# A graph layer on one core: ScalarE's bank clear and VectorE's x sum change places in the step

## The reference

```python
edge_index = jnp.stack([src, dst])
h = jnp.maximum(_layernorm(x, axis=-1), 0.0)          # x: 12500 x 128
# inside the layer, with h in the place of x:
agg_edge = segment_sum(edge_attr, dst, 12500)         # 200000 x 48, dst sorted
collected = concatenate([h, agg_edge], axis=1)        # 176 wide
h1 = silu(collected @ W1 + b1)                        # 256 wide
h2 = silu(h1 @ W2 + b2)
new = h + (h2 @ W3 + b3)
return x + new
```

## Time and profile before

| | |
|---|---|
| Time, median of 3 runs | 332.24 us (332.16 to 332.84) |
| The profiled execution's own time | 331.64 us |
| Its span, first to last instruction | 329.7 us |
| TensorE busy | 311.4 us (94%) |
| VectorE busy | 248.7 us (75%) |
| ScalarE busy | 225.5 us (68%) |
| GpSimd busy | 42.7 us (13%) |
| Mean DMA rate | 161 GB/s |
| Mean granted TensorE clock | 0.990 |

### The profile page before, as it was taken

The page is one execution under the profiler, slowest core; times in us unless marked ns, Lnnn a source line. Parts: engine busy times, 40 slices in busy tenths (PEclk is TensorE's granted clock), DMA queues, the critical chain, the costliest instruction groups (busy, mean ns, idle before and its releaser), DMA issues.

```text
span 329.7 us, 12673 instructions
## 1 busy us (share of the span) xinstructions
PE 311.4 (94%) x4760; PEld 275.2 (83%) x4761; DVE 248.7 (75%) x611; ACT 225.5 (68%) x435; POOL 42.7 (13%) x45
## 2 busy tenths in 40 slices
PE   5767999999999999999999999999999999999994
PEld 5755898889888898889888988898888888898884
DVE  7887877878787878787787778777878686975551
ACT  8864567756776668665875678667856686669752
POOL 4031311001110111011101111011101110111000
PEclk9995999999999999999999999999999999999999
DMA  6993654575447744675367534763467437711112
GB/s 175 305 299 112 195 165 112 179 225 187 114 148 222 218 112 126 213 222 148 101 197 223 176 109 160 223 207 103 141 216 223 134 104 215 221 47 46 32 28 53
DMA packets 79209, 53.04 MB, mean 161 GB/s; under 512 B 2928, under 2 KB 78794, under 8 KB 79184
## 3 DMA queue, kind: packets, MB, share of 16 engines
q1 hardware_dynamic: 79184, 52.70, 53.6%
HBM read 46.29 MB, written 6.40 MB: 160 GB/s over the span
## 4 chain that ended last, share of the span: by engine, by line
PE 79%; DVE 9%; ACT 4%; issue 4%; DVEq 1%; DMA 1%; POOL 1%; SPq 0%; ACTq 0%; POOLq 0%
PE agg_ps L948 18%; PE z L1030 16%; PE z L1014 6%; PE z L994 6%; PE z L1015 5%; PE z L1018 4%; PE agg_ps L965 4%; PE z L999 4%; PE z L1000 4%; PE z L995 4%; PE z L996 4%; PE stage L952 3%; PE tp L978 2%; DVE out_t L829 2%; DVE agg L788 2%
## 5 line engine op out<-in xcount | busy, mean ns | idle before, releaser
L948 PEld LDWEIGHTS agg_ps<-onehot,raw 128*48 128x48 f32 x1568 | 73.1, 125 | 11.7 <-issue 11.7
L650 DVE TENSOR_TENSOR onehot<-window,rel 128x1176 f32<-128x1176 f32 (+1 forms) x57 | 77.2, 1355 | 2.0 <-ACT rel L441 1.2
L948 PE MATMUL agg_ps<-onehot,raw 128*48 128x42 f32 x1568 | 76.8, 214 | 1.7 <-DVE onehot L650 1.7
L952 PE MATMUL stage<-onehot,raw 128*48 128x42 f32 x1560 | 76.5, 214 | 0.0
L952 PEld LDWEIGHTS stage<-onehot,raw 128*48 128x48 f32 x1560 | 72.7, 125 | 0.0
L410 POOL TENSOR_TENSOR rstd<-vareps,minus_half 112x4 f32<-112x4 f32 (+1 forms) x28 | 38.9, 1389 | 260.3 <-DVE vareps L635 260.3
L1030 PE MATMUL z<-w,h 128*112 128x128 f32 (+1 forms) x448 | 56.2, 278 | 1.3 <-ACT h L507 0.8
L1030 PEld LDWEIGHTS z<-w,h 128*112 128x112 f32 (+1 forms) x448 | 50.5, 176 | 3.1 <-ACT z L499 1.1
L812 DVE TENSOR_TENSOR h_lo<-h,h_hi 128x448 fp32r<-128x448 f32 (+1 forms) x56 | 34.9, 624 | 18.0 <-ACT h_hi L521 9.1
L478 ACT ACTIVATE xn<-x_t,nmr,rstd 112x128 f32<-112x128 f32 (+1 forms) x112 | 45.8, 479 | 1.3 <-DVE nmr L643 1.3
L829 DVE TENSOR_TENSOR out_t<-z,resid 112x512 f32<-112x512 f32 (+1 forms) x28 | 19.4, 692 | 34.8 <-PE z L1030 34.8
(11 more groups left out here) (112 smaller groups left out, 445.2 us busy)
## 6 DMA issues: line engine op xcount, KB each, us to landing
raw<-in_edge_attr_dram SPq DMA_DIRECT2D x55, 672.0 KB, 5.1
x_t<-in_x_dram SPq DMA_DIRECT2D x27, 224.0 KB, 3.3
out_dram<-out_t SPq DMA_DIRECT2D x27, 224.0 KB, 3.2
dst_rows<-in_dst_dram SPq DMA_DIRECT2D x1, 512.0 KB
raw<-in_edge_attr_dram SPq DMA_DIRECT2D x1, 288.0 KB, 3.7
dst_rows<-in_dst_dram SPq DMA_DIRECT2D x1, 256.0 KB, 3.0
out_t<-in_L_gnn_W_dram SPq DMA_DIRECT2D x1, 256.0 KB, 7.1
raw<-in_edge_attr_dram SPq DMA_DIRECT2D x1, 192.0 KB, 2.4
```

The costliest lines, as they stand in the source:

```text
L650: return dve.tensor_tensor(onehot[:, slot, at * PER:n * PER, :], window[:, :].unsqueeze(1).broadcast_to([P, cols_n, WINDOW]), cols.unsquee ...
L948: mm = pe.matmul(banks[0:ED, bass.ds(offsets[k - first], WINDOW)], edges, into, start=False, stop=True, skip_group_check=True, tile_positi ...
L952: mm = pe.matmul(stage[ROW2:ROW2 + ED, pair * WINDOW:(pair + 1) * WINDOW], edges, into, start=(k == first and j == 0), stop=True, skip_gro ...
```

## The change

In ScalarE's step `clear_bank` moves from ahead of `activate2` (layer 2's two SiLUs) to behind it. In VectorE's step `add_x` moves from the head of the step to behind `agg_lo`; step 1, where it already stood later, comes out in the order it had. Nothing is added or taken out.

```diff
@@ ScalarE, step(i, parity)
                 if has(i, 1, NT):
                     split_agg(i - 1)
+                if has(i, 2, NT):
+                    activate2(i - 2)
                 if has(i, 1, NT - 2):
                     act.wait_ge(s_carried, i)
                     clear_bank(1 - parity)
-                if has(i, 2, NT):
-                    activate2(i - 2)
                 if has(i, 1, NT):
                     activate1(i - 1)
@@ VectorE, step(i, parity)
                 if has(i, 1, NT):
                     first = isinstance(i, int) and i == 1
-                    if not first:
-                        add_x(i - 1, 1 - parity)
                     carry_over(i - 1, 1 - parity)
                     relu_lo(i - 1)
                     agg_lo(i - 1)
                     if first:
                         make_onehot(2, 0, 1)
                         shift_of_norm(1, 1)
-                        add_x(0, 0)
+                    add_x(i - 1, 1 - parity)
                 if has(i, -2, NB):
                     make_onehot(i + 2, parity, 0)
```

## The result

The changed kernel takes **321.88 us** (median of 4 runs, 321.40 to 322.63) against 332.20 us for the kernel before (4 runs): a ratio of 0.969, 95% interval 0.9665 to 0.9716. That is 3.1% faster. The prediction was 325.2 us with a range of 322.4 to 331.5; the time lies 0.5 us under the range and 0.9 us under the second rival (the gate is gone and the load hides, 322.8).

The account below looks back on a forecast made before the run. TensorE was taken as bound, losing 9.4 us waiting for layer 2's SiLU ahead of layer 1. Gain 9.4 - 1.8 - 0.6 = 7.0 us; 331.64 became 324.6, plus 0.60 for the median: 325.2 us, range 322.4 to 331.5.

Parts of the forecast that it names:

- the second rival: VectorE's x load takes 2.7 us or less and hides; TensorE's whole 9.4 us is gained, 322.8 us; chance 24%.
- The gate ahead of layer 1: TensorE's layer 1 waits for layer 2's SiLU on ScalarE: 0.48 us in the step read, 9.4 us over 26 steps.
- The third rival: At TensorE's layer 1, only the matmuls' visible 2.2 us wait goes, the rest being the sequencer's own: 330.0 us; chance 15%.
- The clear and add_x as edits: On the VectorE-ScalarE path to layer 1, either edit alone shortens it by about the 0.48 us lost; the moved clear costs nothing.
- the ring's length: VectorE's loop from finish through add_x, x load and statistics back to finish: 10.5 us against TensorE's 10.37.
- 7.7 + L: VectorE's loop from finish to finish: 7.7 us plus the x load's time L, taken as 2.8 us.
- given back: Part of the gain lost to VectorE's late x load: 1.8 us in 18 loop steps, 0.6 in eight others.
- the first term: On VectorE, from finish to the moved add_x: 0.79 + 1.95 = 2.74 us.
- The part behind the load: On VectorE, from statistics to nmr 3.77 us, then nmr itself 0.15 us, up to the next finish.
- The 0.6 us for the eight steps outside the loop: In the eight steps written out, late x loads in a few of them cost an estimated 0.6 us.
- The gate's price: TensorE's loss ahead of layer 1: 12.0 - 26 x 0.10 = 9.4 us, 0.36 a step.
- The first rival: The later x load, at L = 3.3 us, makes VectorE the bound: 4 us slower, 336 us; chance 14%.

Follow-up runs that it names:

- the last experiment: The changed kernel with the clear one place later still, behind layer 1's SiLUs and high parts: 402.87 us, ratio 1.2115.
- experiment three: The changed kernel with one added VectorE operation of add_x's size on spare buffers, ahead of add_x in each step: 331.90 us, ratio 0.9978 to the kernel before.
- the changed kernel again: The changed kernel timed once more without any edit, as the measure for other runs of the same chip: 322.38 us, ratio 0.9694 to the kernel before.

## Why the prediction was wrong

**What bounds the kernel: right.** The gate ahead of layer 1 was the loss, and it was 12.0 us of idle weight port that measured it, not the 2.2 us of waiting matmuls. The working gave a step of 10.37 us, and the step is 10.36. What came is the second rival, to which the prediction gave 24 in 100: the whole gate is gained and the load hides. The third rival (only the visible 2.2 us go) is out, and with it the reading of "issue" as the sequencer's own time.

**The clear and add_x as edits: right.** The clear costs nothing behind layer 2's SiLUs, and the last experiment shows by its loss that the room is real and ends soon behind them. Either edit alone gives nearly everything.

**The step that failed is the ring's length**, "7.7 + L ... the ring is then 10.5 against TensorE's 10.37", from which 1.8 us in the loop and 0.6 us outside were given back. The runs showed 10.2, so TensorE stayed the bound. Measured in the changed kernel, VectorE's and SyncE's timelines answer to the earlier trace rows:

```profile
151.28 0.68 DVE L829 TENSOR_TENSOR out_t<-z,resid 112x512 f32<-112x512 f32 x1
...
153.82 0.69 DVE L819 SCALAR_TENSOR_TENSOR resid<-xn,x_t 112x512 f32<-112x512 f32 x1
...
157.70 0.87 DVE L625 BATCH_NORM_STATS2 stats<-x_t 112x6 f32<-112x128 f32 x4 [1.89 <-DMA x_t<-in_x_dram]
...
161.48 0.15 DVE L643 SCALAR_TENSOR_TENSOR nmr<-meanvar,rstd 112x4 f32<-112x4 f32 x1
161.55 0.68 DVE L829 TENSOR_TENSOR out_t<-z,resid 112x512 f32<-112x512 f32 x1
...
164.10 0.69 DVE L819 SCALAR_TENSOR_TENSOR resid<-xn,x_t 112x512 f32<-112x512 f32 x1
...
167.97 0.87 DVE L625 BATCH_NORM_STATS2 stats<-x_t 112x6 f32<-112x128 f32 x4 [1.89 <-DMA x_t<-in_x_dram]
...
172.07 0.68 DVE L829 TENSOR_TENSOR out_t<-z,resid 112x512 f32<-112x512 f32 x1
...
182.10 0.68 DVE L829 TENSOR_TENSOR out_t<-z,resid 112x512 f32<-112x512 f32 x1
```

```profile
154.70 0.34 SPq L317 DMA_DIRECT2D x_t<-in_x_dram  x1
...
164.99 0.34 SPq L317 DMA_DIRECT2D x_t<-in_x_dram  x1
```

Rounds alone do not give the ring's own length: TensorE paces them, and over the loop they average its step (151.28 to 192.70, the `finish` after those shown, is four rounds of 10.36). Their terms do, and so does experiment three, 10.22. In the first round the terms are 2.54 from `finish` to `add_x`, 0.88 to the issue, 3.00 for the load and 3.78 + 0.07 from the statistics to the next `finish`. In the second they are 2.55, 0.89, 2.98 and 4.10; the two kinds of round alternate, with the two halves of the loop's body. The load was not over-estimated: I took 2.8, and from issue to the start of the statistics it is 3.00 here and 2.83 on average in the loop, with a median to landing over the span of 2.7, against 3.3 before:

```profile
x_t<-in_x_dram SPq DMA_DIRECT2D x27, 224.0 KB, 2.7
```

Over-estimated was the rest. I took 2.74 for the first term, from rows in which `finish` is followed by `add_x` 0.79 us later; `carry_over` follows it after 0.60 (three operations on, 153.82 - 151.28 = 2.54). I carried over the 1.12 us between `add_x` and the issue in every other step; it is 0.87 to 0.89 in the loop. The part behind the load I had nearly right: 3.77 + 0.15 against 3.85 and 4.10 by turns. And the 0.05 for the loop's register operations had no row behind it. Without the load the two rounds are 7.27 and 7.54, 7.4 on average, where I had 7.7. With that and the same 2.8 the ring is 10.2, there is some 0.15 us of room, and nothing is given back. The 0.6 us for the eight steps outside the loop had no row behind it either; the changed kernel without any such loss fits the time.

**The gate's price was 0.9 us too low.** The sum took 0.36 us a step, from the weight port's idle time less an allowance. Layer 3 starts in the loop, before and after (the chains):

```profile
66.34 1.94 PE z L1030 x16
...
249.14 1.93 PE z L1030 x16
```

```profile
65.80 1.93 PE z L1028 x16
...
241.98 1.93 PE z L1028 x16
```

That is 17 steps each, 182.80 us before and 176.18 after: 0.39 a step, 10.1 us in 26 steps. The span of the profiled executions fell by only 9.6 because the one of the changed kernel was slower in its first microseconds, which the change does not touch. The first of these lines is from before, the second from after:

```profile
5.19 0.49 DVE rel_rows L598
```

```profile
5.93 0.49 DVE rel_rows L598
```

In the profile of "the changed kernel again" this operation starts at 5.29, and its span is 319.6, 10.1 under the one before. Between the medians the gain is 10.3. So the miss of 3.3 us is 2.4 (given back, not real) and 0.9 (the gate gave 10.3 for 9.4). The second of these put the time outside the range: its low end, 322.4, already gave nothing back, and allowed only 0.4 us for a larger gate. That it fell 0.5 us outside is little against the 1.2 us by which the four runs of the changed kernel differ.

**The first rival** (the later x load makes VectorE the bound) has the right mechanism: 0.61 us more in the ring turned 321.9 us into 331.9. Its price and place were wrong, since the ring was 0.3 us shorter than the 10.5 I had.

## What to carry to other kernels

Where two operations stand one behind the other between a late producer and a waiting TensorE, moving either may give nearly the whole gain; time each alone before counting both. A ring through several engines and a DMA is priced from start to start of neighbouring operations, with no term taken from an operation that waited; a few tenths of a microsecond too many made a free edit look like a quarter of the gain. And when an operation is moved out of the way, ask for the last place where it is still free: one place further on cost 80 us here.

## What the runs showed of the hardware

The wait ahead of a weight load costs TensorE more than the profile's idle time of its matmuls: the matmuls were credited with 2.2 us of waiting in 9 steps, the weight port with 12.0 in 26, and some 10 us were gained when the wait was gone. The Trainium skill, TensorE: Matmul & The Clock Gate, section Step-by-step: what each phase is for, has weight loads pulled ahead of running matmuls; the trace agrees in the undisturbed case, with the load 0.19 us ahead of its matmul in the changed kernel. In the kernel before, where the load had to wait for the SiLU, it stood only 0.03 us ahead.

With the clear in the wrong place TensorE stood still for 1.9 us of the step read, and its granted clock fell from 1.00 (2.4 GHz) to 0.50 (1.2 GHz) and stayed there for the 3 us that followed. The next step waited as long and kept 1.00; in that kernel's loop two steps in three lost the clock. I had priced the wait alone; the slower sums behind it added 1.4 us to the step read.
